# TensorE takes a task between the last pooled products of a pair and the next skip term, and tables of steps and shares change with it

## The chip, the cores and the metric

The kernel runs on one core of one Trainium2 chip. The core has TensorE (PE, matmuls), VectorE (DVE), ScalarE (ACT), GpSimd (POOL) and SyncE (SP, which issues most DMAs here). Each works through its own list of instructions in order, and they meet at semaphores. The metric is the device time of one execution in microseconds (us); lower is better.

## What is computed

The reference is one layer of a network on x of 2 sequences x 2048 rows x 512 features, in float32:

```python
h = _layernorm(x) * (1 + ca) + sa
x = x + ga * mixer(h)
h = _layernorm(x) * (1 + cb) + sb
x = x + gb * ffn(h)            # one 512 x 512 product, the sum of 8 factors, and a bias

# mixer, E = 1024 channels, N = 16 states, 4 taps
h, gate = split(h @ in_proj_w.T)
h = silu(conv4(h) + conv_b)                  # along the sequence
dt, Bp, Cp = split(h @ x_proj_w.T)           # 128, 16 and 16 columns
dt = softplus(dt @ dt_proj_w.T + dt_proj_b)
s[t] = s[t-1] * exp(dt * A) + (dt * h) * Bp  # the scan, for each channel and state
y = sum over states of s * Cp
y = (y + h * D) * silu(gate)
return y @ out_proj_w.T
```

## The kernel before

**Rounds, units, quads, pairs and steps.** The rows are cut into 16 chunks of 256 rows, and a round works on one chunk (8 chunks for each sequence). A round scans 1024 channels x 16 states. A unit is one state of a pair of channel tiles (128 partitions x 2 x 256 rows). There are 64 units in a round: 4 pairs (`q`) of 16 units. Four units make a quad, two units make a step `s`, so a round has 32 steps and 16 quads, and a pair has 8 steps. Pairs begin at steps 0, 8, 16 and 24.

**A unit's way through the engines.** ACT writes exp(dt * A) into one of three PSUM banks (`decays`, L722). POOL has made the inputs of a whole quad (`make_ub`, L568). DVE scans (`scan`, L1426). The state is then multiplied by C. A table gives each quad the number of its units that POOL multiplies (`EVEN_POOL` for even chunks, `ODD_POOL` for odd ones; `FIRST_POOL`, `FOLD_POOL` and `LAST_POOL` for chunks 0, 1 and 15). These are the last units of the quad: DVE scans them into `state_p`, and POOL multiplies them in one instruction for the quad (L596). The others stay in the bank, and DVE multiplies them into the ring `sc_d` (L1441). ACT copies the last column of every state to `carry` (L706) before the bank is used again, and clears the bank's middle column (L718) where DVE had used the bank for a product. TensorE adds the products over the 16 states by transposing them into one PSUM bank, `y_bank` (L1010). A new pair starts that bank with the skip term h * D (`turn_skip`, L1001), and for that ACT must have copied the finished sums of the pair before it (`copy_y`, L811), which waits for POOL's last products of that pair to be turned.

**The two side streams.** Between the scans of round c the engines do the second half of chunk c-1 (gate, sums, output projection, FFN), which the code marks `lc`, and the first half of chunk c+1 (input projection, taps, dt, B and C), marked `la`. TensorE's part of them is in `one_round` (L1307 on): 

- `project_gate` (L1057) makes the gate's columns, ACT takes their tanh (`tanh_gate`, L859) and DVE multiplies (`silu_gate`, L1500).
- `turn_sums` (L1141) turns the sums of a pair, and DVE multiplies the gate by them (`gate_sums`, L1522).
- `project_out` (L1157) is the output projection, which DVE adds to x (`residual_mixer`, L1529).
- `project_h` (L1085) makes one of eight input tiles at the steps in `IN_AT`, two for each pair of channel tiles. With a pair complete, ACT copies it for the taps and applies the last tap and the bias (`copy_h`, L766 to L775), DVE adds one tap (`taps`, L1481), TensorE the other two (`add_tap`, L1068, `ADD_AT`), ACT takes the tanh (`tanh_before`, L787) and DVE multiplies (`silu_before`, L1490, both at `SILU_AT`). In the kernel before, `copy_h` on ACT and `taps` on DVE are both ruled by `TAP_AT`.

The second numbers of these tables hold for rounds 1 and later. The order of work on an engine is the order in which `one_round` of that engine calls these functions. Within a step of TensorE it is: `add_tap`, the turns of the products (`turn_states`), the side work for chunk c+1, the side work for chunk c-1. Within a step of ACT it is: the decays of two units, with `copy_y` and a few others between, then `skip`, the work for chunk c+1, and last `tanh_gate`. So `tanh_gate(3)` at step 5 stands behind `copy_h(0)` of the next chunk.

## Time and profile before

| | us |
|---|---|
| median of 3 runs | 2022.62 |
| lowest to highest | 2021.11 to 2022.76 |
| the profiled execution | 2025.55 |
| its span, first to last instruction | 2023.8 |
| first scan starts at (from the span's start) | 60.5 |
| rounds 2 to 14, start of the first to start of round 15 | 325.8 to 1878.1 |
| last scan starts at | 1992.5 |

Busy time in the span: DVE 1867.4 us (92%), POOL 1835.7 (91%), PE 1759.7 (87%), ACT 1517.1 (75%).

The rows further down are of this one execution. A row of the timeline says when an instruction (or a row of like ones, xcount) began, how long it was busy, and in square brackets how long its engine had been idle before it and whose work ended the idle time. Each DVE instruction is counted as busy some 0.09 us into the next one: scans that follow each other start 1.19 us apart, and a product 0.59 us before the next instruction. TensorE's groups overlap likewise: four transposes of one unit take 0.43 us from start to start, an input or gate tile 1.73, half an output row tile (L1157 x4) 1.72. Where these distances are used, they are differences of start times in the rows.

### The profile page before, as it was taken

Reading aid. Unit: us, or ns where it says so; the run is one execution under the profiler, and the core shown is the slowest. Engines: PE = TensorE matmul, PEld = TensorE weight load, DVE = VectorE, ACT = ScalarE, POOL = GpSimd, SP = SyncE. Lnnn points to the kernel's source line nnn. Section 1 sums busy time; section 2 is a strip of 40 time slices with the busy share of each in tenths; the row PEclk is TensorE's granted clock in tenths of the full one; section 3 lists DMA queues with packets and bytes.
Section 4 is the critical chain, followed back from the end, with each engine's and each line's share of the span. In section 5 each row is a group of like instructions: output and inputs, shape, how many; then the busy total and the mean of one; then the engine's idle time right before and its main releaser. Section 6 shows DMA issues by size and latency. Waiting matters only on the chain.

```text
span 2023.8 us, 29343 instructions
## 1 busy us (share of the span) xinstructions
PE 1759.7 (87%) x9128; PEld 1312.2 (65%) x9128; DVE 1867.4 (92%) x2240; ACT 1517.1 (75%) x4646; POOL 1835.7 (91%) x925
## 2 busy tenths in 40 slices
PE   7985889889889898988989888898988899898798
PEld 5664757667576765757666675766757576676564
DVE  2799989999999999999999999999999999999995
ACT  3767778697877869777786977878787786878662
POOL 1789999999999999999998999999999999999992
PEclk9897999999999999999999999999999999999798
DMA  4656514132140412304042240403223040311200
GB/s 171 235 114 153 140 48 147 31 121 79 43 143 15 152 47 97 103 30 154 17 141 68 111 141 22 157 22 131 68 73 121 28 156 22 121 53 55 92 27 32
DMA packets 72001, 186.17 MB, mean 92 GB/s; under 512 B 6818, under 2 KB 8482, under 8 KB 63908
## 3 DMA queue, kind: packets, MB, share of 16 engines
q1 hardware_dynamic: 68148, 176.95, 26.3%
q0 software_dynamic: 3696, 7.34, 2.2%
q8 instruction: 73, 1.20, 0.2%
q14 instruction: 84, 0.69, 0.1%
HBM read 172.20 MB, written 12.06 MB: 91 GB/s over the span
## 4 chain that ended last, share of the span: by engine, by line
PE 42%; ACT 19%; POOL 15%; DVE 13%; issue 9%; DMA 1%; DVEq 0%; POOLq 0%; SPq 0%; ACTq 0%
PE y_bank L1010 10%; PE bank_a L1085 10%; PE bank_c L1157 9%; POOL ub L568 8%; ACT decay L722 7%; DVE decay L1426 5%; POOL state_p L596 5%; PE bank_c L1057 4%; DVE state_p L1426 3%; PE bank_a L1068 2%; ACT dt L835 2%; DVE sc_d L1441 2%; ACT L722 2%; ACT hT L737 2%; ACT L835 2%
## 5 line engine op out<-in xcount | busy, mean ns | idle before, releaser
L568 POOL TENSOR_TENSOR ub<-u,b_all 128x2048 f32<-128x2048 f32 x255 | 1160.4, 4551 | 48.5 <-DMA b_all<-bc_scratch 47.4
L722 ACT ACTIVATE decay<-dt,decay_rate 128x256 f32<-128x256 f32 (+1 forms) x2048 | 889.6, 466 | 36.0 <-DVE state_p L1426 34.3
L1426 DVE TENSOR_TENSOR_SCAN decay<-decay,carry,ub 128x512 f32<-128x512 f32 x610 | 763.7, 1277 | 25.8 <-ACT decay L722 23.8
L596 POOL TENSOR_TENSOR state_p<-state_p,c_all 128x1024 f32<-128x1024 f32 (+1 forms) x256 | 498.7, 1948 | 85.3 <-ACT carry L706 82.4
L1426 DVE TENSOR_TENSOR_SCAN state_p<-decay,carry,ub 128x512 f32<-128x512 f32 x414 | 527.4, 1274 | 9.3 <-ACT decay L722 7.2
L1010 PE MATMUL y_bank<-ident,sc_d 128*128 128x128 f32 x2440 | 362.5, 283 | 79.9 <-DVE sc_d L1441 79.5
L1441 DVE TENSOR_TENSOR sc_d<-decay,c_all 128x512 f32<-128x512 f32 x610 | 406.7, 671 | 0.0
L1010 PEld LDWEIGHTS y_bank<-ident,sc_d 128*128 128x128 f32 x2440 | 292.9, 145 | 146.1 <-DVE sc_d L1441 120.8
L706 ACT ACTIVATE carry<-decay 128x2 f32<-128x2 f32 x610 | 100.8, 165 | 264.8 <-DVE sc_d L1441 262.9
L1010 PEld LDWEIGHTS y_bank<-ident,state_p 128*128 128x128 f32 x1656 | 195.7, 143 | 126.9 <-POOL state_p L596 71.7
L1010 PE MATMUL y_bank<-ident,state_p 128*128 128x128 f32 x1656 | 231.0, 279 | 53.2 <-POOL state_p L596 52.0
L1085 PE MATMUL bank_a<-hT,win_h 128*128 128x256 f32 x992 | 240.5, 387 | 32.4 <-DVE hc L1490 30.0
L1057 PE MATMUL bank_c<-hT,win_z 128*128 128x256 f32 x960 | 230.7, 387 | 0.0
L1157 PE MATMUL bank_c<-wo,yg 128*128 128x512 f32 x480 | 223.8, 594 | 0.0
L1085 PEld LDWEIGHTS bank_a<-hT,win_h 128*128 128x128 f32 x992 | 182.3, 193 | 58.7 <-DVE hc L1490 35.7
L1057 PEld LDWEIGHTS bank_c<-hT,win_z 128*128 128x128 f32 x960 | 181.7, 196 | 22.6
L1068 PE MATMUL bank_a<-pre_z,tap_diag 128*128 128x256 f32 x496 | 120.4, 386 | 12.2 <-DVE bank_a L1481 12.2
L1157 PEld LDWEIGHTS bank_c<-wo,yg 128*128 128x128 f32 x480 | 86.6, 191 | 67.0 <-issue 64.8
L1068 PEld LDWEIGHTS bank_a<-pre_z,tap_diag 128*128 128x128 f32 x496 | 92.7, 191 | 39.8 <-DVE bank_a L1481 15.8
L1187 PE MATMUL bank_c<-ffn,hT 128*128 128x512 f32 x240 | 115.9, 605 | 0.0
L1001 PE MATMUL y_bank<-ident,skipped 128*128 128x128 f32 x256 | 42.9, 294 | 71.5 <-ACT y_rows L811 71.5
L718 ACT ACTIVATE decay<-ident 128x1 f32<-128x1 f32 x608 | 103.4, 170 | 0.1
(139 smaller groups left out, 1842.1 us busy)
## 6 DMA issues: line engine op xcount, KB each, us to landing
win_h<-win_m SPq DMA_DIRECT2D x128, 256.0 KB, 2.6
win_z<-win_m SPq DMA_DIRECT2D x128, 256.0 KB, 2.8
b_all<-bc_scratch SPq DMA_DIRECT2D x31, 1024.0 KB, 4.7
c_all<-bc_scratch SPq DMA_DIRECT2D x31, 1024.0 KB, 6.6
xa<-x SPq DMA_DIRECT2D x16, 512.0 KB, 5.0
xc<-x SPq DMA_DIRECT2D x16, 512.0 KB, 3.8
out<-xc SPq DMA_DIRECT2D x15, 512.0 KB, 4.0
ffn<-factors POOLq DMA_DIRECT2D x7, 1024.0 KB, 10.0
```

The lines of the kernel that those rows point to most:

```text
L568: pool.tensor_tensor(ub[:, slot, :, :, :], u[:, (PAIRS * c + q) % U_PAIRS, :, :].unsqueeze(1).to_broadcast([P, QUAD, 2, ROWS]), b_all[:, n ...
L596: pool.tensor_tensor(part, part, c_all[:, n + QUAD - k:n + QUAD, :].unsqueeze(2).to_broadcast([P, k, 2, ROWS]), ALU.mult).then_inc(pooled, 1)
L718: act.activation(bk[:, ROWS:ROWS + 1], ident[:, 0:1], ACT.Copy, scale=0.0)
L722: last = act.activation(bk[:, j * ROWS + j:(j + 1) * ROWS], dt[:, pair % DT_PAIRS, j, j:], ACT.Exp, scale=decay_rate[:, e, n:n + 1])
L1010: last = pe.matmul(y_bank[:, at:at + P], tile[:, j, t * P:(t + 1) * P], ident[:, :], start=False, stop=last_of_pair, is_transpose=True, sk ...
L1057: last = pe.matmul(dst[:, j * ROWS:(j + 1) * ROWS], tile[:, k, :], hTc[:, k, :], start=(k == 0), stop=(k == KD - 1))
L1068: last = pe.matmul(h_lane(c, q)[:, j * ROWS:(j + 1) * ROWS], tap_diag[:, i, 2 * q + j, :], pre[q % 2][:, j, k:k + ROWS], start=False, stop ...
L1085: last = pe.matmul(h_lane(c, q)[:, j * ROWS:(j + 1) * ROWS], win_h[i % H_TILES][:, k, :], hT[c % H_RING][:, k, :], start=(k == 0 and j == ...
L1157: last = pe.matmul(bank_c[t][:, :], yg[:, k, t * P:(t + 1) * P], wo[:, k, :], start=(k == 0), stop=(k == KE - 1))
L1187: last = pe.matmul(bank_c[t][:, :], hT[c % H_RING][:, k, t * P:(t + 1) * P], ffn[:, k, :], start=False, stop=(k == KD - 1))
L1426: dve.tensor_tensor_scan(dst, bk[:, :], ub[:, quad % UB_RING, i, :, :].rearrange("p j r -> p (j r)"), carried_in[:, n, 2 * q:2 * q + 1], A ...
L1441: dve.tensor_tensor(sc_d[:, i % D_RING, :, :], bk[:, :].rearrange("p (j r) -> p j r", j=2), c_all[:, n:n + 1, :].to_broadcast([P, 2, ROWS] ...
```

## The change

Six things change; the number of instructions of each kind is the same.

1. On TensorE `turn_states` is split. The turn of POOL's products of the quad before (`turn_finished`) comes first. At steps 1, 9, 17 and 25, where a pair ends, one task follows it before the skip term: `project_gate(c-1, 2, 1)`, `project_out(c-1, 0, 0)`, `project_dt(c+1, 1)`, and the bias with the first product of `project_ffn(c-1, 1)`. At step 0 the gate tile also comes ahead of the turns.
2. In the rest of a step TensorE does the work for chunk c-1 ahead of that for chunk c+1, where it was the other way round.
3. In rounds 1 and later the first four input tiles come a step earlier (steps 1 to 4 for 2 to 5).
4. On ACT `tanh_gate` comes right behind the step's decays.
5. `copy_h` gets a table of its own, equal to the old `TAP_AT`. DVE's taps of pairs 2 and 3 come a step later (12 and 14), TensorE's too (13 and 15), and the tanh and silu that follow (15 and 17).
6. The tables of POOL's share are spread otherwise: quads 3 and 7 (the last of pairs 0 and 1) go from 2 to 1, quad 12 from 1 to 2, in even chunks quad 8 from 2 to 3, in odd chunks quad 4 from 1 to 2. The sums stay 27 and 26 units.

```diff
-IN_AT = ((2, 3, 4, 5, 7, 8, 9, 10), (2, 3, 4, 5, 8, 9, 10, 11))
...
+IN_AT = ((2, 3, 4, 5, 7, 8, 9, 10), (1, 2, 3, 4, 8, 9, 10, 11))
+COPY_AT = ({5: 0, 7: 1, 10: 2, 12: 3}, {5: 0, 7: 1, 11: 2, 13: 3})
+TAP_AT = ({5: 0, 7: 1, 10: 2, 12: 3}, {5: 0, 7: 1, 12: 2, 14: 3})
...
-EVEN_POOL = (2, 2, 2, 2, 2, 2, 2, 2, 2, 2, 2, 1, 1, 1, 1, 1)
...
+EVEN_POOL = (2, 2, 2, 1, 2, 2, 2, 1, 3, 2, 2, 1, 2, 1, 1, 1)
...
                     decays(2 * step + 1)
...
+                    if lc is not None and s in (1, 3, 5):
+                        tanh_gate(c - 1, {1: 1, 3: 2, 5: 3}[s])
...
-                        if a in TAP_AT[c > 0]:
-                            copy_h(c + 1, TAP_AT[c > 0][a])
+                        if a in COPY_AT[c > 0]:
+                            copy_h(c + 1, COPY_AT[c > 0][a])
...
+            def turn_finished(step):
+
+                quad = step // 2
+                if step % 2 and quad:
+                    turn_on_pool(quad - 1)
+
             def turn_states(step):
 
                 quad = step // 2
                 first = quad % (N // QUAD) == 0
-                if step % 2 and quad:
-                    turn_on_pool(quad - 1)
...
+                    turn_finished(STEPS * c + s)
+                    if lc is not None:
+                        if s <= 1:
+                            project_gate(c - 1, 2, s)
+                        if s == 9:
+                            project_out(c - 1, 0, 0)
+                        if s == 25:
+                            ffn_bias(c - 1, 1)
+                            project_ffn(c - 1, 1, (0,))
+                    if la is not None and s == 17:
+                        project_dt(c + 1, 1)
                     turn_states(STEPS * c + s)
```

What the order of the instructions shows follows for round 4, an even one. The numbers behind the names are those of the buffers; in these rows a transposed unit is x4.

TensorE from step 9 to step 11, at the start of pair 1, before (L1085 is an input tile, L1157 the output projection, L1001 the skip term, `state_p` POOL's products, `sc_d` DVE's):

```order
L1010 MATMUL y_bank<-ident,state_p 128x128 x8
L1001 MATMUL y_bank<-ident,skipped 128x128 x4
L1010 MATMUL y_bank<-ident,sc_d 128x128 x8
L1085 MATMUL bank_a0<-hT2,win_h0 128x256 x4
L1157 MATMUL bank_c0<-wo,yg 128x512 x2
L1010 MATMUL y_bank<-ident,sc_d 128x128 x4
L1085 MATMUL bank_a1<-hT2,win_h1 128x256 x4
L1157 MATMUL bank_c0<-wo,yg 128x512 x2
L1010 MATMUL y_bank<-ident,state_p 128x128 x8
L1010 MATMUL y_bank<-ident,sc_d 128x128 x4
L1085 MATMUL bank_a1<-hT2,win_h2 128x256 x4
L1157 MATMUL bank_c0<-wo,yg 128x512 x2
```

The same place in the changed kernel, whose lines are 1 to 5 further down (L1011, L1002, L1090, L1162):

```order
L1011 MATMUL y_bank<-ident,state_p 128x128 x4
L1162 MATMUL bank_c0<-wo,yg 128x512 x2
L1002 MATMUL y_bank<-ident,skipped 128x128 x4
L1011 MATMUL y_bank<-ident,sc_d 128x128 x8
L1090 MATMUL bank_a0<-hT2,win_h0 128x256 x4
L1011 MATMUL y_bank<-ident,sc_d 128x128 x4
L1162 MATMUL bank_c0<-wo,yg 128x512 x2
L1090 MATMUL bank_a1<-hT2,win_h1 128x256 x4
L1011 MATMUL y_bank<-ident,state_p 128x128 x8
L1011 MATMUL y_bank<-ident,sc_d 128x128 x4
L1162 MATMUL bank_c0<-wo,yg 128x512 x2
L1090 MATMUL bank_a1<-hT2,win_h2 128x256 x4
```

The first output projection stands ahead of the skip term, POOL's part is one unit instead of two, and the last input tile (L1090, win_h2) has three output projections ahead of it in this piece instead of two.

DVE from step 12 to step 14, before (L1426 scan, L1441 product, L1481 the tap of pair 3, L1490 the silu of pair 2):

```order
L1426 SCALAR_TENSOR_TENSOR decay1<-decay1,carry0,ub 128x512
L1426 SCALAR_TENSOR_TENSOR decay2<-decay2,carry0,ub 128x512
L1441 TENSOR_TENSOR sc_d<-decay1,c_all 128x512
L1426 SCALAR_TENSOR_TENSOR state_p<-decay0,carry0,ub 128x512
L1441 TENSOR_TENSOR sc_d<-decay2,c_all 128x512
L1426 SCALAR_TENSOR_TENSOR state_p<-decay1,carry0,ub 128x512
L1481 SCALAR_TENSOR_TENSOR bank_a1<-pre_z,conv,bank_a1 128x256 x2
L1426 SCALAR_TENSOR_TENSOR decay0<-decay0,carry0,ub 128x512
L1426 SCALAR_TENSOR_TENSOR decay2<-decay2,carry0,ub 128x512
L1441 TENSOR_TENSOR sc_d<-decay0,c_all 128x512
L1490 SCALAR_TENSOR_TENSOR hc<-tanh_s,bank_a0 128x512
```

And in the changed kernel (L1438, L1453 and L1493 are the scan, the product and the tap):

```order
L1438 SCALAR_TENSOR_TENSOR decay2<-decay2,carry0,ub 128x512
L1438 SCALAR_TENSOR_TENSOR decay0<-decay0,carry0,ub 128x512
L1453 TENSOR_TENSOR sc_d<-decay2,c_all 128x512
L1493 SCALAR_TENSOR_TENSOR bank_a0<-pre_z,conv,bank_a0 128x256 x2
L1438 SCALAR_TENSOR_TENSOR state_p<-decay1,carry0,ub 128x512
L1453 TENSOR_TENSOR sc_d<-decay0,c_all 128x512
L1438 SCALAR_TENSOR_TENSOR state_p<-decay2,carry0,ub 128x512
L1438 SCALAR_TENSOR_TENSOR decay1<-decay1,carry0,ub 128x512
L1438 SCALAR_TENSOR_TENSOR decay0<-decay0,carry0,ub 128x512
L1453 TENSOR_TENSOR sc_d<-decay1,c_all 128x512
L1493 SCALAR_TENSOR_TENSOR bank_a1<-pre_z,conv,bank_a1 128x256 x2
```

The tap of pair 3 went from ahead of step 14's first scan to the end of step 14, and the tap of pair 2 from step 11 to step 12.

ACT at step 5, from the decays of unit 11 on, before (L766 to L775 are `copy_h(0)`, L859 is `tanh_gate(3)`):

```order
L722 ACTIVATE decay1<-dt,decay_rate 128x255
L766 ACTIVATE pre_z<-hist0 128x2x3
L767 ACTIVATE pre_z<-bank_a0 128x2x256
L770 ACTIVATE hist0<-bank_a0 128x6
L775 ACTIVATE bank_a0<-bank_a0,conv 128x256 x2
L859 ACTIVATE tanh_s<-bank_c1 128x512
L722 ACTIVATE decay0<-dt,decay_rate 128x256
```

ACT at the same place in the changed kernel (L860 is `tanh_gate(3)`, L767 to L776 are `copy_h(0)`):

```order
L723 ACTIVATE decay1<-dt,decay_rate 128x255
L860 ACTIVATE tanh_s<-bank_c1 128x512
L767 ACTIVATE pre_z<-hist0 128x2x3
L768 ACTIVATE pre_z<-bank_a0 128x2x256
L771 ACTIVATE hist0<-bank_a0 128x6
L776 ACTIVATE bank_a0<-bank_a0,conv 128x256 x2
L723 ACTIVATE decay0<-dt,decay_rate 128x256
```

The tanh moved from behind the copies to ahead of them. At step 13 ACT's rows are the same in both kernels: `copy_h(3)`, and right behind it the decays of unit 28.

## Rows read from the trace of the kernel before

**Rows 1.** Windows view, rounds 2 to 14: length, busy us (instructions), clock, DMA.

```profile
325.80:1878.10 1552.30, 1375.38 (x7336) 1037.46 (x7334) 1491.44 (x1783) 1224.10 (x3753) 1473.49 (x736) 0.99 0.26 86
```

**Rows 2.** Waits view, DVE, rounds 2 to 14: us in total, times, longest us.

```profile
DVE yg L1500 <- ACT tanh_s L859: 15.6, 13, 1.9
DVE xc L1529 <- PE bank_c L1157: 12.3, 13, 0.9
DVE decay L1426 <- ACT decay L722: 11.9, 33, 1.3
DVE bank_a L1481 <- ACT bank_a L775: 9.5, 13, 0.9
DVE yg L1522 <- PE bank_c L1141: 5.3, 13, 0.4
```

**Rows 3.** Timeline of DVE, round 7 (from 921.2): start, busy us, [idle before].

```profile
942.40 0.69 DVE L1500 SCALAR_TENSOR_TENSOR yg<-tanh_s,bank_c 128x512 f32<-128x512 f32 x1 [1.89 <-ACT tanh_s L859]
...
956.34 0.68 DVE L1490 SCALAR_TENSOR_TENSOR hc<-tanh_s,bank_a 128x512 f32<-128x512 f32 x1
...
974.44 0.88 DVE L1481 SCALAR_TENSOR_TENSOR bank_a<-pre_z,conv,bank_a 128x256 f32<-128x256 f32 x2 [0.67 <-ACT bank_a L775]
975.23 2.47 DVE L1426 TENSOR_TENSOR_SCAN decay<-decay,carry,ub 128x512 f32<-128x512 f32 x2
...
989.88 0.69 DVE L1529 TENSOR_TENSOR xc<-bank_c,xc 128x512 f32<-128x512 f32 x1 [0.95 <-PE bank_c L1157]
```

**Rows 4.** Timeline of PE in round 7, steps 8 to 16.

```profile
957.07 1.99 PE L1085 MATMUL bank_a<-hT,win_h 128*128 128x256 f32 x8 [2.15 <-DVE hc L1490]
958.90 1.04 PE L1010 MATMUL y_bank<-ident,state_p 128*128 128x128 f32 x8
960.71 0.63 PE L1001 MATMUL y_bank<-ident,skipped 128*128 128x128 f32 x4 [0.78 <-ACT y_rows L811]
961.18 1.47 PE L1010 MATMUL y_bank<-ident,sc_d 128*128 128x128 f32 x12
962.49 1.89 PE L1085 MATMUL bank_a<-hT,win_h 128*128 128x256 f32 x8
964.22 1.88 PE L1157 MATMUL bank_c<-wo,yg 128*128 128x512 f32 x4
...
972.42 1.88 PE L1157 MATMUL bank_c<-wo,yg 128*128 128x512 f32 x4
...
986.24 3.60 PE L1157 MATMUL bank_c<-wo,yg 128*128 128x512 f32 x8
```

**Rows 5.** Timeline of ACT in round 7, step 13 and the decays behind it.

```profile
972.62 0.21 ACT L766 ACTIVATE pre_z<-hist 128x6 f32<-128x6 f32 x1 [0.70 <-PE bank_a L1085]
...
974.33 0.87 ACT L722 ACTIVATE decay<-dt,decay_rate 128x256 f32<-128x256 f32 x2
```

**Rows 6.** Timeline of PE at pair 0's start: round 6, then round 7.

```profile
811.09 1.89 PE L1057 MATMUL bank_c<-hT,win_z 128*128 128x256 f32 x8
...
928.17 0.63 PE L1001 MATMUL y_bank<-ident,skipped 128*128 128x128 f32 x4 [2.04 <-ACT y_rows L811]
...
930.08 3.00 PE L1057 MATMUL bank_c<-hT,win_z 128*128 128x256 f32 x8
```

**Rows 7.** Timeline of DVE in round 6 at step 5.

```profile
822.34 0.69 DVE L1500 SCALAR_TENSOR_TENSOR yg<-tanh_s,bank_c 128x512 f32<-128x512 f32 x1 [0.40 <-ACT tanh_s L859]
```

**Rows 8.** Timeline of PE in round 3 at step 8.

```profile
478.46 3.60 PE L1085 MATMUL bank_a<-hT,win_h 128*128 128x256 f32 x8 [2.14 <-DVE hc L1490]
```

**Rows 9.** Windows view of that stretch, columns as in rows 1.

```profile
478.00:482.00 4.00, 3.54 (x9) 2.84 (x10) 4.00 (x6) 1.41 (x5) 4.00 (x3) 0.57 0.00 0
```

**Rows 10.** Timeline of DVE: round 1 at step 26, then round 7 at step 22.

```profile
305.32 1.29 DVE L1426 TENSOR_TENSOR_SCAN decay<-decay,carry,ub 128x512 f32<-128x512 f32 x1 [0.95 <-ACT decay L722]
...
1004.59 2.47 DVE L1426 TENSOR_TENSOR_SCAN decay<-decay,carry,ub 128x512 f32<-128x512 f32 x2 [0.40 <-ACT decay L722]
```

**Rows 11.** Waits view, POOL, rounds 2 to 14.

```profile
POOL state_p L596 <- ACT carry L706: 57.9, 55, 2.8
```

More of the change, by code:

```diff
@@ L57 @@
 DT_PAIRS = 5
-EVEN_POOL = (2, 2, 2, 2, 2, 2, 2, 2, 2, 2, 2, 1, 1, 1, 1, 1)
-ODD_POOL = (2, 2, 2, 2, 1, 2, 2, 2, 2, 2, 2, 1, 1, 1, 1, 1)
+EVEN_POOL = (2, 2, 2, 1, 2, 2, 2, 1, 3, 2, 2, 1, 2, 1, 1, 1)
+ODD_POOL = (2, 2, 2, 1, 2, 2, 2, 1, 2, 2, 2, 1, 2, 1, 1, 1)
 FIRST_POOL = (2, 2, 1, 1, 1, 1, 1, 2, 1, 1, 1, 1, 1, 1, 1, 1)
@@ L1322, in one_round @@
                             pe.wait_ge(rows_made, 2 * BATCH)
[L1323 to L1338 removed]
                     if lc is not None:
[L1340 to L1341 removed]
+                        if s in (2, 3):
+                            project_gate(c - 1, 3, s - 2)
                         if 4 <= s <= 7:
                             turn_sums(c - 1, s - 4)
[L1344 to L1345 removed]
+                        if 10 <= s <= 12:
                             project_out(c - 1, 0, s - 9)
@@ L1365, in one_round @@
                             project_ffn(c - 1, 1, (3,))
+                    if la is not None:
+                        if c == 0 and s == 3:
+                            turn_x(1, 0)
+                            turn_x(1, 1)
+                        if a in IN_AT[c > 0]:
+                            i = IN_AT[c > 0].index(a)
+                            project_h(c + 1, i // 2, i % 2)
+                        if s in (16, 18, 19):
+                            project_dt(c + 1, s - 16)
+                        if s in (18, 19):
+                            project_b_c(c + 1, s - 18)
+                        if s == 20:
+                            project_b_c(c + 1, 2)
+                            project_b_c(c + 1, 3)
+                        if s in (22, 23, 26, 27):
+                            expand_dt(c + 1, s - 22 - 2 * (s // 26))
                     if c + 2 < CHUNKS and s == 31:
```

30 lines of the change are left out of this document (2 added, 28 removed).

## The prediction

> **What bounds the kernel now.** I read the windows view first. In rounds 2 to 14 DVE is busy 1491.4 of 1552.3 us, and its line in the waits view adds up to nearly all of the rest, so a round of 119.4 us is DVE's own work plus DVE's waits [rows 1, 2]. A change that moves work and adds none can gain only from these waits. There are 55.9 us of them over 13 rounds, 4.3 in a round, and the timeline says where they stand [rows 2, 3]:
> - Step 5, the third gate product waits for ACT's tanh: 15.6 us in all, 1.89 in one kind of round and 0.40 in the other [rows 2, 3, 7].
> - Step 6, a gate sum waits for TensorE: 5.3 us [rows 2].
> - Step 13, the tap of pair 3 waits for ACT's copy: 9.5 us [rows 2, 3].
> - Step 17, the second residual waits for TensorE's output projection: 12.3 us, 0.95 in each round [rows 2, 3].
> - Scans that wait for decays: 13.2 us, of which 4.2 stand at step 10 and 7.8 at steps 22 and 23, and one of 1.3 in round 14 [rows 2, 10]. (The line of 11.9 and one more of 1.3; I sorted them by the number of scans ahead of them.)
>
> POOL waits 57.9 us for ACT's carries in the same rounds and never holds a scan up, since no line of DVE's waits names it [rows 2, 11].
>
> **Part 1: the tanh ahead of the copies (step 5), and gate work first on TensorE.** In round 6 the copies took ACT 1.7 us ahead of the tanh, as they do at step 13 (972.62 to 974.33), and DVE waited 0.40 [rows 5, 7]. With the tanh first, it is done 1.7 us sooner and the 0.40 is gone. In round 7 the wait was 1.89. There TensorE's gate tile at step 1 took 2.83 us from start to start (3.00 busy) against 1.72 (1.89 busy) in round 6, behind an idle gap of 2.04 at the skip term [rows 6]; it and the gap held back the input tile that ACT's copy waits for. The input tiles come one step earlier now and the gate tile goes into the gap, so both parts of the 1.89 go: 15.6 us in 13 rounds. The copy behind the tanh then ends about when DVE has done the gate product, 0.59 after its start; I take nothing for it and up to 0.3 us a round as bound. At step 6 the turned sums no longer stand behind input tiles (1.73 each), so the 5.3 goes. Half of the 4.2 at step 10 or more goes with POOL's lighter quad 3: ACT's copy of the sums waited there for a turn of two units that is now one, 0.43 sooner; I take all of it.
>
> **Part 2: from step 8 to step 17.** Here TensorE works without a gap from the first silu on: the input tile begins 0.05 us after the silu ends (957.02, that is 956.34 + 0.68), and the last output projection ends as the residual begins, 32.9 us later [rows 3, 4]. The gap at the skip term is 0.94 us from start to start (the turn of two units takes 0.87, 958.90 to 960.71 is 1.81) [rows 4]. The output projection (1.72) fills it, and TensorE's end moves to 31.9 after the silu. That alone would be worth 0.94 a round. But the order shows something that works against it: the eighth input tile at step 11 now stands behind a third output projection. Before, it ended at 972.42, which is 15.40 after the silu [rows 4]. Now 1.72 more are ahead of it, 0.94 less of gap, and 0.43 less of POOL's turn (quad 3 has one unit; in odd rounds quad 4 has one unit less for DVE's turns and one more for POOL's, which cancels): 15.40 + 1.72 - 0.94 - 0.43 = 15.75. ACT copies at step 13 only when this tile is there; it had already waited 0.70 for it [rows 5]. ACT's copy takes 1.71, and right behind it in ACT's list are the decays of unit 28, 0.87 more [rows 5]. So the scan of unit 28 can't begin before 15.75 + 0.20 + 1.71 + 0.90 = 18.56 after the silu; in the kernel before it was 18.21 (975.23) [rows 3]. The tap of pair 3 used to stand ahead of that scan and covered its wait, with 0.67 of waiting and 0.79 of work from 974.44 to 975.23 [rows 3]. It has moved behind, and so has nothing to cover with. DVE arrives at the scan at 18.21 - 0.67 - 0.79 - 0.59 (one product less in quad 4) = 16.16 in odd rounds, and at 18.21 - 0.67 - 0.79 - 0.50 (the wait at step 10) = 16.25 in even ones. **A new wait of about 2.3 us** takes the place of the one of 0.73, under another name: a scan that waits for ACT's decays. From there to the residual DVE had 13.7 us of work (975.23 to 989.88 less 0.95) [rows 3]. It gets the tap (+0.79) and quad 7's third product (+0.59), and the last silu goes behind the residual (-0.59); even rounds lose a product in quad 8 (-0.59). The residual then begins at 32.5 in even and 33.0 in odd rounds, later than TensorE's 31.9. So the wait of 0.95 at step 17 goes, and TensorE's saving at the gap is worth nothing there.
>
> The Trainium skill, TensorE: Matmul & The Clock Gate, "Architectural detail", says that ScalarE and VectorE are strict FIFOs. It speaks against putting work ahead of the eighth tile; without it ACT could make the decays while it waits for the tile, and the sum would be 1975.7 us. The trace agrees with the rule: the decays behind ACT's 0.70 wait began only when the copies were done [rows 5].
>
> **Part 3: the rest.** TensorE's gaps at steps 17 and 25 and ACT's stall behind the copy of the sums at step 18 get shorter, but no wait of DVE follows them, so they are worth nothing. The last silu at step 17 adds 0.59 behind the residual, and quad 12's second pooled unit takes 0.59 off. The 0.6 a round at steps 22 and 23 stays: ACT has the same list there [rows 10]. Quads 3 and 7 now have three DVE products in a row; the row nearest to that is step 22, where such a quad begins and waits 0.40 plus 0.20 [rows 10]. In quads 3 and 7 DVE also has gate sums, taps or a silu between its scans, which gives ACT time, so I take 0, with 0.6 a quad as the bound. POOL's three units in quad 8 cost it one more unit, and it has 57.9 / 13 = 4.5 us a round of waits [rows 11].
>
> **Sum.** Gone in rounds 2 to 14: 15.6 + 5.3 + 4.2 + 9.5 + 12.3 = 46.9 us. New: 13 x 2.3 = 29.9. Net 17.0. Round 0 has other tables, rounds 1 and 15 and the tail I take as unchanged. Of the profiled execution (2025.55, span 2023.8) this makes 2008.5; the median of the runs lies 2.9 below the profiled one, so **2022.6 - 17.0 = 2005.6 us**. The terms can move it by 4 for 0.3 a round at step 5, 5 for 0.4 in the new wait, 3 in round 1: 1996 to 2015.
>
> **Rivals.**
> - *The new wait does not come, and TensorE bounds the stretch.* If the eighth tile is not as late as worked out (the taps' order or ACT's lead may differ), the residual begins at TensorE's 31.9. DVE would reach it after 30.2 us in even rounds (32.9 less waits of 2.1, less 0.59) and 30.7 in odd ones, so it waits 1.5 on average, 19.9 in all: 46.9 - 19.9 = 27, **1995.6**. For: the 0.35 us by which the scan moves is small. Against: ACT's list at step 13 is the same, and that chain already set the scan.
> - *The clock's fall moves into the stretch that TensorE bounds.* In 7 of the 13 rounds the slow gate tile of rows 6 stands behind the 2.04 gap. With that gap filled, the longest gap is the 2.15 at step 8 [rows 4]. It happened there once: in round 3 the input tile behind it took 3.60 busy instead of 1.99 at a mean granted clock of 0.57, so mostly at the lower level of 1.2 GHz instead of 2.4, 1.6 us lost [rows 4, 8, 9]. Seven such rounds cost 11.2: **2016.8**. Against: one in 13 so far. The same page of the Trainium skill says in its Part 1 that the default is throttled and that activity releases it, which makes idle gaps the cause, as rows 6 and 8 do.
> - *Quads 3 and 7 stall (the other side).* A bank that held a DVE product is free only when ACT has copied its carry and cleared it. If ACT can't keep pace in the two new quads of three products, each costs the 0.6 of rows 10, 15.6 in all: 2021.2, no change. In round 1 a scan waited 0.95 in such a stretch [rows 10]. At 0.95 a quad it is 24.7: **2030.3**, slower. It turns slower from 0.81 a quad, (2026.7 - 2005.6) / 26. For: ACT has the skip and the copies at steps 6 and 7. Against: DVE's extras there.
> - *POOL becomes the bound.* Its waits of 4.5 us are for ACT's carries. If they stay where they are, the round stays at 119.4: **2022**.
>
> **Chances.** A measurement can tell about 0.2%, 4.0 us. Forecast 0.46, TensorE's bound 0.17, clock 0.15 (all three faster: 0.78); quads 3 and 7 0.16, of which 0.07 is within 0.2% and 0.09 slower; POOL 0.06, the same. Faster 0.78, same 0.13, slower 0.09. The range reaches over the first three cases with their bounds and to the edge of no change: 1989 to 2022.
>
> **What would show it.** In the waits of DVE, the lines for `yg` on the tanh and on TensorE's turned sums and for the tap on ACT's copy vanish. The line of scans on ACT's decays grows from 11.9 to some 35 us, with the new entries at the first scan of step 14. The residual's wait goes to 0; if it stays near 1.5 a round and step 14 has no wait, the first rival holds. Slow tiles at a clock below 1 at step 8 show the second, waits at steps 7 to 9 and 15 to 17 the third. TensorE's 0.78 at the skip terms of steps 9 and 17 should be gone in any case. It would all be wrong if DVE had come to wait for something that has no line now, such as POOL's inputs.

## The result, and the profile after

The changed kernel takes **2043.43 us** (median of 4 runs, 2036.58 to 2049.72) against 2022.69 (2021.11 to 2022.83) for the kernel before on the same chip: ratio 1.0102, 95% interval 1.0076 to 1.0128. It is slower by 1%, where 2005.6 was forecast and 2022 was the end of the range. Its profiled execution is its fastest, 2036.58 (span 2034.8), and the 15.4 us by which rounds 2 to 14 grew can be placed in it (1567.70 against 1552.30). The whole profiled execution grew by only 11.0, since what lies outside these rounds, which the forecast took as unchanged, is 4.4 shorter. One execution of the run with the old tables of POOL's share further down took 3837 us and is left out of that run's median. In this section line numbers are those of the changed kernel: L1438 is the scan, L1453 DVE's product, L1493 the tap, L1541 the residual, L1011 the turns, L1002 the skip term, L1090 an input tile, L1128 the expansion of dt.

The windows view of rounds 2 to 14 (length; busy us and instructions of PE, PEld, DVE, ACT, POOL; clock) answers to [rows 1]:

```profile
324.60:1892.30 1567.70, 1395.18 (x7334) 1042.66 (x7333) 1488.17 (x1783) 1224.52 (x3752) 1473.73 (x735) 0.98 0.26 85
```

DVE does the same work (1488.2 us, it was 1491.4). PE does the same work too and is busy 20 us more, at a mean clock of .98 instead of .99. DVE's waits over the same rounds answer to [rows 2]:

```profile
DVE decay L1438 <- ACT decay L723: 56.5, 55, 1.8
DVE state_p L1438 <- ACT decay L723: 19.4, 17, 2.4
```

The four lines of `yg`, `xc` and `bank_a` are gone, as forecast. What is left are scans that wait for decays, 75.9 us in all where some 35 were forecast and 55.9 was the total before. DVE's timeline of round 7 (step 10, step 14, the second residual at step 17, step 25) answers to [rows 3]:

```profile
970.77 1.29 DVE L1438 TENSOR_TENSOR_SCAN decay<-decay,carry,ub 128x512 f32<-128x512 f32 x1 [0.80 <-ACT decay L723]
...
986.04 2.47 DVE L1438 TENSOR_TENSOR_SCAN decay<-decay,carry,ub 128x512 f32<-128x512 f32 x2 [1.84 <-ACT decay L723]
...
1000.45 0.66 DVE L1541 TENSOR_TENSOR xc<-bank_c,xc 128x512 f32<-128x512 f32 x1
...
1029.43 1.28 DVE L1438 TENSOR_TENSOR_SCAN state_p<-decay,carry,ub 128x512 f32<-128x512 f32 x1 [0.98 <-ACT decay L723]
```

And PE's timeline, first round 4 at step 8 and at step 18, then round 7 at step 18:

```profile
600.97 2.71 PE L1090 MATMUL bank_a<-hT,win_h 128*128 128x256 f32 x8 [2.15 <-DVE hc L1502]
...
640.71 1.12 PE L1011 MATMUL y_bank<-ident,sc_d 128*128 128x128 f32 x4 [3.11 <-DVE sc_d L1453]
641.62 1.92 PE L1107 MATMUL bank_a<-hc,xp 128*128 128x256 f32 x4
...
1006.22 0.66 PE L1011 MATMUL y_bank<-ident,sc_d 128*128 128x128 f32 x4 [3.27 <-DVE sc_d L1453]
1006.72 1.03 PE L1107 MATMUL bank_a<-hc,xp 128*128 128x256 f32 x4
```

At that place the kernel before had a gap of 0.42 us, here its round 7:

```profile
995.14 0.66 PE L1010 MATMUL y_bank<-ident,sc_d 128*128 128x128 f32 x4 [0.42 <-DVE sc_d L1441]
```

The same instruction at step 18 (a turn x4, then a projection x4) takes 0.66 and 1.03 us in round 7 and 1.12 and 1.92 in round 4, twice the time at the same size. The windows view of the two stretches in round 4 has the granted clock in the column behind the busy times:

```profile
600.90:604.40 3.50, 3.43 (x13) 2.89 (x14) 3.50 (x5) 0.87 (x2) 3.50 (x2) 0.67 0.00 0
640.70:645.30 4.60, 4.59 (x12) 2.46 (x12) 4.60 (x7) 4.55 (x15) 4.52 (x4) 0.50 0.00 0
```

0.50 is the lower of TensorE's two levels, 1.2 GHz instead of 2.4, and 0.67 a mixture of both. Each such **fall of the clock** in rounds 2 to 14 comes behind a gap of TensorE. I cut a round into three stages: from its first scan to the end of the first silu at step 8 (stage 1), from there to the second residual (stage 2), and from the residual to the end of the last scan (stage 3). They show what a fall costs, since rounds of one kind, even or odd, differ in little else:

| us | before | changed |
|---|---|---|
| stage 1, no fall | 34.17 | 33.79 |
| stage 1, fall behind the 2.04 gap of step 1 | 35.85 (7 rounds of 13) | none |
| stage 2, no fall | 32.87 | 32.34 even, 32.94 odd |
| stage 2, fall behind the 2.15 gap of step 8 | 34.47 (1 round) | 34.02 even, 34.62 odd (9 rounds) |
| stage 3, no fall | 50.27 | 50.87 (50.82 to 51.13 in 6 rounds) |
| stage 3, fall behind the gap of 3.11 or 3.27 at step 18 | none | 52.1 to 53.7 (7 rounds) |

Summed over the 13 rounds: the clock took 11.8 + 1.6 = 13.4 us before and takes 9 x 1.68 = 15.1 at step 8 and 13.6 at step 18 now, 15.3 more. All the rest together (-4.9 in stage 1, -3.2 in stage 2, +8.3 in stage 3) is 0.2. So in this reading the order of the work gained nothing, and the clock lost all of the 15.4. The experiments put both halves to the test.

### The profile page after: what moved, and what is told of

The parts are those of the page before. It is cut to its first block and busy times, and to the rows that moved or that the text cites. A ratio compares the mean times of both kernels' runs of the same rounds, so it can differ in the third digit from the quotient of the medians.

```text
span 2034.8 us, 29343 instructions
## 1 busy us (share of the span) xinstructions
PE 1773.9 (87%) x9128; PEld 1310.7 (64%) x9128; DVE 1864.1 (92%) x2240; ACT 1517.3 (75%) x4646; POOL 1836.4 (90%) x925
## 5 line engine op out<-in xcount | busy, mean ns | idle before, releaser
L1438 DVE TENSOR_TENSOR_SCAN decay<-decay,carry,ub 128x512 f32<-128x512 f32 x610 | 764.2, 1277 | 70.8 <-ACT decay L723 68.7
L597 POOL TENSOR_TENSOR state_p<-state_p,c_all 128x1024 f32<-128x1024 f32 (+2 forms) x256 | 498.6, 1948 | 98.1 <-ACT carry L707 89.3
L1438 DVE TENSOR_TENSOR_SCAN state_p<-decay,carry,ub 128x512 f32<-128x512 f32 x414 | 526.4, 1273 | 25.2 <-ACT decay L723 24.4
L1011 PE MATMUL y_bank<-ident,sc_d 128*128 128x128 f32 x2440 | 360.0, 279 | 154.3 <-DVE sc_d L1453 154.1
L1011 PEld LDWEIGHTS y_bank<-ident,sc_d 128*128 128x128 f32 x2440 | 282.5, 142 | 213.7 <-DVE sc_d L1453 194.8
L1453 DVE TENSOR_TENSOR sc_d<-decay,c_all 128x512 f32<-128x512 f32 x610 | 407.3, 670 | 2.5 <-PE y_bank L1011 2.5
L1011 PE MATMUL y_bank<-ident,state_p 128*128 128x128 f32 x1656 | 237.9, 284 | 45.6 <-POOL state_p L597 45.4
L1090 PE MATMUL bank_a<-hT,win_h 128*128 128x256 f32 x992 | 246.1, 393 | 32.4 <-DVE hc L1502 30.0
L1011 PEld LDWEIGHTS y_bank<-ident,state_p 128*128 128x128 f32 x1656 | 200.8, 146 | 104.5 <-POOL state_p L597 63.2
L1090 PEld LDWEIGHTS bank_a<-hT,win_h 128*128 128x128 f32 x992 | 188.9, 196 | 74.3 <-DVE hc L1502 35.7
L1162 PE MATMUL bank_c<-wo,yg 128*128 128x512 f32 x480 | 229.8, 607 | 0.0
L1062 PE MATMUL bank_c<-hT,win_z 128*128 128x256 f32 x960 | 226.1, 381 | 0.0
L1062 PEld LDWEIGHTS bank_c<-hT,win_z 128*128 128x128 f32 x960 | 175.1, 191 | 19.7
L1162 PEld LDWEIGHTS bank_c<-wo,yg 128*128 128x128 f32 x480 | 86.3, 198 | 67.7 <-issue 67.7
L1073 PEld LDWEIGHTS bank_a<-pre_z,tap_diag 128*128 128x128 f32 x496 | 92.6, 191 | 33.3 <-issue 13.4
L546 POOL TENSOR_TENSOR u<-dt,hc 128x512 f32<-128x512 f32 x63 | 80.4, 1276 | 0.0
```

The lines of the kernel that those rows point to most:

```text
L597: pool.tensor_tensor(part, part, c_all[:, n + QUAD - k:n + QUAD, :].unsqueeze(2).to_broadcast([P, k, 2, ROWS]), ALU.mult).then_inc(pooled, 1)
L1011: last = pe.matmul(y_bank[:, at:at + P], tile[:, j, t * P:(t + 1) * P], ident[:, :], start=False, stop=last_of_pair, is_transpose=True, sk ...
L1062: last = pe.matmul(dst[:, j * ROWS:(j + 1) * ROWS], tile[:, k, :], hTc[:, k, :], start=(k == 0), stop=(k == KD - 1))
L1073: last = pe.matmul(h_lane(c, q)[:, j * ROWS:(j + 1) * ROWS], tap_diag[:, i, 2 * q + j, :], pre[q % 2][:, j, k:k + ROWS], start=False, stop ...
L1090: last = pe.matmul(h_lane(c, q)[:, j * ROWS:(j + 1) * ROWS], win_h[i % H_TILES][:, k, :], hT[c % H_RING][:, k, :], start=(k == 0 and j == ...
L1162: last = pe.matmul(bank_c[t][:, :], yg[:, k, t * P:(t + 1) * P], wo[:, k, :], start=(k == 0), stop=(k == KE - 1))
```

## The experiments

The theory at the start: the time was lost to falls of the clock, and a fall belongs to the gap before it. The first rival: the falls come with the chip or the run, and the new waits of DVE (steps 14 and 25) are the loss. The means is a filler: TensorE transposes a tile of zeros into a sum that is open, which adds nothing to it and makes a gap shorter. Ratios are to runs of the kernel before on the same chip (medians of 2021.4 to 2023.9 on the three chips used), with the 95% interval in brackets; where two experiments stand side by side, they may be of different chips. Line numbers are those of each run's own kernel: the scan is L1450 in one and L1454 in another.

**Both gaps of the changed kernel filled.**

```
+                    if la is not None and s == 8:
+                        add_zeros(y_bank, 16)
+                    if la is not None and s == 17:
+                        add_zeros(y_bank, 24)
```

where `add_zeros` is, in short, `pe.matmul(bank[:, 0:P], zero, ident, start=False, stop=False, is_transpose=True)` in a loop.

> The changed kernel with TensorE kept busy in two of its gaps: 16 transposes of a tile of zeros, added to the sums of the pair (which they leave as they are), at the end of step 8's turns, and 24 at the end of step 17's, in rounds 0 to 14. Clock theory: the changed kernel loses its time to falls of TensorE's clock behind the gaps of 2.15 us at step 8 (9 of 13 rounds, 1.7 us each) and of 3.1 us before step 18's turn (7 of 13 rounds, 1.2 to 2.7 us each). Without them a round is 117.3 us as in its undisturbed rounds instead of 120.6, so the whole is 43 us less than the profiled 2036.6: 1990 to 2000 us, no slow tile at steps 8 and 18 in rounds 2 to 14. Order theory (the lists of ACT and TensorE alone cost the time): no gain, 2036 to 2050 us or a little more for the added work.

Measured: **2011.5 us** (2010.65 to 2012.3), ratio .9939 [.9924, .9954], and no fall in rounds 2 to 14. 32 us came off the changed kernel by work that computes nothing, and the rounds are those that had no fall before (33.78, 32.33 or 32.93, 50.87 to 51.14), so these stages show no other effect of the filler. The waits of DVE at steps 14 and 25 stayed, here over rounds 2 to 14:

```profile
DVE decay L1450 <- ACT decay L725: 33.5, 39, 1.8
DVE state_p L1450 <- ACT decay L725: 15.2, 13, 2.4
```

48.7 us, of which 24.0 at step 14 and 15.2 at step 25. So the fillers are worth 32 us in the median (more than the 15.3 of the profiled execution, which was the fastest of four; the others had a clock of .966, .963 and .960). My lower figure of 1990 to 2000 missed, since I had added the three stages up and left out the 1.1 us between a round's last scan and the next round's first.

**Only the gap of step 8 filled** (the first two lines of that diff).

> The same filler at step 8 alone. Clock theory: the falls at step 8 go (9 x 1.7 = 15 us), those behind the 3.1 us gap at step 18 stay and may be more: 2015 to 2030 us, the stretch from the first silu to the second residual is 32.3 us in even and 32.9 in odd rounds in every round. Order theory: no gain.

Measured: **2027.7 us** (2022.82 to 2029.23), 1.0016 [1.0007, 1.0025]. There was no fall at step 8 any more, but there were falls at step 18 in 12 of 13 rounds, where the unfilled kernel had 7. Round 7, which had none there, now reads:

```profile
995.52 1.12 PE L1013 MATMUL y_bank<-ident,sc_d 128*128 128x128 f32 x4 [3.27 <-DVE sc_d L1463]
996.43 1.91 PE L1115 MATMUL bank_a<-hc,xp 128*128 128x256 f32 x4
```

**The kernel before, its gap of step 1 filled** (`add_zeros(bank_c[0], 16)` ahead of the skip term). This is what the change itself does to that gap, and nothing else.

> The kernel before with its gap of 2.04 us at step 1 filled: 16 transposes of zeros ahead of the skip term of pair 0, added to a gate tile, in rounds 1 to 15. Clock theory: the 7 slow gate tiles of rounds 2 to 14 go, 1.5 us each, 10.7 us: 2012 us, if the fall does not move to the gap of 2.15 us at step 8, where each costs 1.6; if it moves there in 9 of 13 rounds, 2022.7 + 14.4 - 10.7 = 2026 us. Order theory: within 2 us of 2022.7.

Measured: **2023.0 us** (2020.35 to 2025.55), .9999 [.9989, 1.0008]. The gap is gone and so are its falls, and they come back at step 8 in 8 of 13 rounds. Round 7, first the skip term [rows 6], then step 8 [rows 4]:

```profile
928.09 0.63 PE L1003 MATMUL y_bank<-ident,skipped 128*128 128x128 f32 x4 [0.29 <-ACT y_rows L813]
...
955.32 2.98 PE L1095 MATMUL bank_a<-hT,win_h 128*128 128x256 f32 x8 [2.15 <-DVE hc L1500]
```

The gap of 2.15 had stood there before, and the tile behind it took 1.99. It takes 2.98 now. A gap that cost nothing in this round cost 1.7 us as soon as an earlier one was closed. The number of falls did not change: the eight rounds (3, 5, 7, 8, 10, 11, 13, 14) are the seven that had one at step 1 and the one that had it at step 8.

**The kernel before, both its gaps filled** (the same, and 16 zeros at step 8).

> The kernel before with both gaps filled: 16 transposes of zeros ahead of the skip term of pair 0 and 16 at the end of step 8's turns. Theory (the clock is the difference between the two kernels, their lists of work are worth the same): no slow tile in rounds 2 to 14, every round 34.2 + 32.9 + 50.3 us in its three stretches, against 33.8 + 32.6 + 51.0 in the changed kernel with its gaps filled, so the whole is within 3 us of that kernel's 2011.5: 2009 to 2014. Rival (the order of the changed kernel has a gain of its own that the clock hides): 2018 or more. Second rival (the fall moves to a third gap): 2015 to 2023, with slow groups at steps 17 to 23.

Measured: **2011.8 us** (2009.69 to 2014.29), .9952 [.9937, .9967], no fall. Here the two orders of work stand side by side without the clock: 2011.8 for the old one and 2011.5 for the new one, on two chips. The ratios (.9952 and .9939) have intervals that overlap, and rounds 2 to 14 take 1538.7 and 1540.0 us. The change is worth nothing clear of the noise when the clock is taken out, as the sum of 0.2 said. The first rival does not explain the loss, but the question moves: four waits went, and where did their gain go?

**The old tables of taps** (`TAP_AT`, `ADD_AT` and `SILU_AT` of before in the changed kernel, no filler).

> The changed kernel with the old tables for the taps, their TensorE part and the silu (11 and 13, 12 and 14, 14 and 16). If the tap of pair 3 covered ACT's late decays, as the prediction has it: the wait at the first scan of step 14 falls from 1.8 us a round to about 1.0 on ACT's copy at step 13, the stretch from the first silu to the second residual in rounds without a fall of the clock is 0.6 to 0.8 us shorter (31.6 in even, 32.2 in odd rounds), and the whole is 8 to 10 us less, 2027 to 2040 us by the number of clock falls. If the place of the tap does not matter: the stretch stays at 32.3 and 32.9 and the time at 2036 to 2050 us.

Measured: **2024.7 us** (2022.61 to 2028.89), 1.0008 [.9999, 1.0017]. The gap of step 18 shrank from 3.1 and 3.3 to between 2.3 and 2.8, and falls there went from 7 rounds to 2; at step 8 there were 8, and one at step 23 behind a gap of 2.03. The tap again covers the wait for the eighth input tile (1.50 at the tap in place of 1.85 at the scan), and stage 2 is 32.15 and 32.75. I had expected 31.6 and 32.2, because I forgot that the last silu then stands ahead of the residual again.

**`project_h` ahead of `project_out` at steps 10 and 11**, in the changed kernel with both gaps filled:

```
+                    early_h = la is not None and lc is not None and s in (10, 11)
+                    if early_h:
+                        i = IN_AT[1].index(s)
+                        project_h(c + 1, i // 2, i % 2)
...
-                        if a in IN_AT[c > 0]:
+                        if a in IN_AT[c > 0] and not early_h:
```

> The changed kernel with both gaps filled and, at steps 10 and 11, the input tile ahead of the output projection again. Theory: the wait of 1.85 us at the first scan of step 14 comes from the eighth input tile, which stands behind one more projection; the tile now ends 1.72 sooner, that wait falls to 0.1 to 0.3, and TensorE's last output projection bounds the stretch instead: the second residual begins 31.9 us after the first silu in even and odd rounds (32.3 and 32.9 before), with a wait of 0.7 to 1.2 at step 17. 0.75 us a round, 10 in all: 2000 to 2004 us. Rival (the wait at step 14 comes from ACT's other work): it stays at 1.85 and the time at 2011.5.

Measured: **2005.1 us** (2004.59 to 2006.07), .9919 [.9904, .9933]. The wait at step 14 is gone and TensorE bounds stage 2 at 31.90 in every round:

```profile
DVE state_p L1454 <- ACT decay L725: 17.5, 13, 2.8
DVE xc L1557 <- PE bank_c L1170: 12.0, 13, 1.2
DVE decay L1454 <- ACT decay L725: 9.8, 28, 0.4
```

That confirms the chain of Part 2 (eighth tile, copy, decays, scan) and prices it: 6.4 us for what stood in the forecast as a wait of 29.9. In the traces stage 2 lost 9.2 us over 13 rounds, and stage 3 took 2.8 of them back, in even rounds: the wait at step 25 grew from 15.2 to 17.5 us.

**The old tables of POOL's share** (both of before), in the changed kernel with both gaps filled.

> The changed kernel with both gaps filled and the old tables of POOL's share. Theory: the second pooled unit of quad 12 leaves DVE without work to cover ACT's softplus at step 25 (a wait of 1.17 us a round that the kernel before does not have); with the old tables that wait goes, and the first scan of step 14 waits about 0.4 more since quad 3's turn on TensorE takes 0.43 more: 0.6 a round less in all, 2002 to 2006 us against 2011.5. Rival (the new tables help, as the lighter last quads bring the sums sooner): slower than 2013.

> The changed kernel with filled gaps and the old tables of POOL's share once more, for its waits: the time of the first runs (2004.7) again. If the table is what lengthens the wait at step 25, it is 0.1 to 0.4 us a round here (1.17 with the new tables), and the first scan of step 14 waits 2.2 instead of 1.85.

Measured: **2004.7 us** (2002.66 to 2005.12), .9914 [.9897, .993]; the trace read here is of the second run of the same kernel, 2003.9. Stage 1 is 33.18 instead of 33.79, one product of DVE (0.59) less in quad 3, and the wait at step 25 is 6.0 us instead of 15.2. The spread of POOL's share that the change brought costs 7 us.

**Quad 12's second unit given to quad 11**, in the changed kernel with both gaps filled, the old taps and `project_h` first.

> The changed kernel with both gaps filled, the input tile first at steps 10 and 11, the old tables for taps, TensorE's taps and silu, and the second pooled unit in quad 11 instead of quad 12. If all theories hold they add up to the point at which TensorE bounds the stretch between steps 8 and 17 (31.9 us less what the silu behind the residual had hidden, so 0.2 to 0.6 more than with the tile alone) and the wait at step 25 (1.17) and those at step 22 (0.39) go: 1990 to 1998 us. If ACT's list is the limit wherever DVE gets lighter, the waits come back at other steps and it is 2000 to 2006.

Measured: **2005.0 us** (2002.93 to 2008.7), .992 [.9904, .9936], a miss. In round 6 PE waited for POOL's products at step 23, the clock fell, and ACT waited for the expansion of dt; round 10 has the same fall. The two cost some 8 us of stage 3 in this execution, the slowest of four. In the other rounds the wait at step 25 is 0.6 or 1.1 us, where `project_h` first alone had 1.0 or 1.6, and new ones of 0.4 to 0.8 stand at step 23, as the second case of the expectation has it. PE's turn, ACT's second softplus, then DVE's scan:

```profile
887.41 1.73 PE L1013 MATMUL y_bank<-ident,state_p 128*128 128x128 f32 x8 [2.27 <-POOL state_p L599]
```

```profile
895.74 0.84 ACT L838 ACTIVATE dt<-bank_a,ch 128x256 f32<-128x256 f32 x2 [4.72 <-PE bank_a L1136]
```

```profile
898.91 1.28 DVE L1454 TENSOR_TENSOR_SCAN state_p<-decay,carry,ub 128x512 f32<-128x512 f32 x1 [4.91 <-ACT decay L725]
```

**Both of the costly parts taken out, gaps filled** (`project_h` first, old taps, old POOL tables; what is left is the task between, the tanh first, the work for chunk c-1 first on TensorE elsewhere, and the earlier input tiles), **and the same without filler.**

> The changed kernel with both gaps filled, the input tile first at steps 10 and 11, and the old tables for POOL's share, the taps and the silu. What is left of the change is the task between POOL's last products and the skip term, the earlier tanh and the earlier input tiles. Theory: the gate stages cost 33.2 us (quad 3's product is back on POOL), TensorE bounds the stretch from the first silu to the second residual at 31.9 + 0.4 (two units in quad 3's turn) = 32.3, the rest 50.3 as in the kernel before. 115.8 + 1.1 a round against 118.46 in the changed kernel with filled gaps: 1988 to 1996 us. Rival (ACT's list at steps 12 to 14 and 22 to 25 takes back what DVE saves): 2000 or more.

> The same without any filler. Clock theory: the lists are better, but the gaps of 2.1 us at step 8 and 2 to 3 us at step 18 are open, so the clock falls in most rounds at one of them: 8 to 13 rounds x 1.7 us at step 8 and some at step 18, 12 to 30 us more than with the filler: 2003 to 2022 us. Order theory: within 3 us of the kernel with the filler.

Measured: **1996.8 us** (1996.53 to 1997.38), .987 [.9855, .9884], and 2013.8 (2009.44 to 2015.1), .995 [.9931, .9969]. The stages are 33.18, 31.90 and 51.1 to 51.3. Without filler the clock falls at step 8 in 8 of 13 rounds again, and the median is 17 us longer; in the profiled executions rounds 2 to 14 are 12.0 longer (1537.8 against 1525.9).

**The part that the change is named after, alone** (`turn_finished` and one task ahead of the skip term at steps 1, 9, 17, 25, in the kernel before, nothing else):

```
+                    turn_finished(STEPS * c + s)
+                    if lc is not None:
+                        if s == 1:
+                            project_gate(c - 1, 2, s)
+                        if s == 9:
+                            project_out(c - 1, 0, 0)
...
```

> The kernel before with one part of the change alone: at steps 1, 9, 17 and 25 the gate tile, the output projection, the dt product and the bias with the first FFN product stand between the turn of POOL's products and the skip term. Tables, ACT's order and the order of the other work are the old ones. Theory: TensorE's gap of 0.78 at the skip terms of steps 9 and 17 and of 2.04 at step 1 go, but DVE is not faster for it: the input tiles at steps 9 to 11 stand 0.8 us later (1.72 less 0.94), so the stretch to the second residual keeps 32.7 us in even and odd rounds, and the fall of the clock moves from step 1 to step 8 in 6 to 10 rounds. 2018 to 2030 us. Rival (the gap was what cost): 0.94 us a round and the slow gate tiles, 10 to 25 us faster, 1998 to 2012.

Measured: **2008.2 us** (2008.03 to 2008.66), .9926 [.9911, .9941]: faster, where I had expected no gain. The stages are 33.95, 31.90 and 50.27, and the falls are as many as in the filled kernel before, 8 of 13 at step 8 (33.57). Part 2 had said so: "That alone would be worth 0.94 a round", and the table has 32.87 and 31.90.

**The same with 16 zeros at step 8.**

> The kernel before with the part that the change is named after alone (another task between POOL's last turns and the skip terms), and beside it sixteen transposes of zeros behind TensorE's turns of step 8, as a filler of the gap there. In the run of that part alone (2008.2 us) the clock fell at step 8 in 8 of 13 rounds, and a round with a fall was 1.67 us longer. Theory (these falls are all that the clock still takes): no fall in rounds 2 to 14, 8 x 1.67 = 13.4 us less, 1994 to 1996 us. Rival (a fall moves on to the next gap, as it did before): falls at steps 17 to 25, 2000 to 2008 us.

Measured: **1993.7 us** (1993.25 to 1995.49), .9857 [.9842, .9871], no fall. It came as the theory said, and the rival (the fall moves on) fell: no gap over 1.88 us is left in these rounds.

**Then the tanh ahead of the copies.**

```
+                    if lc is not None and s in (1, 3, 5):
+                        tanh_gate(c - 1, {1: 1, 3: 2, 5: 3}[s])
```

> The kernel just above, and tanh's gate right behind the decays on ScalarE, as the changed kernel has it. Theory (the wait of .57 us in the first stage of a round is tanh's): that stage falls from 33.95 to 33.4 us, 13 x .57 = 7.4 us, 1987 to 1989 us. Rival (the gate ahead delays ScalarE's later work by as much): the same time as the kernel above within 2 us.

Measured: **1999.9 us** (1999.54 to 2000.05), .9885 [.9869, .9902]. Neither case: 6.2 us slower. Round 7, ACT at step 5, then DVE's first tap:

```profile
931.18 0.60 ACT L861 ACTIVATE tanh_s<-bank_c 128x512 f32<-128x512 f32 x1 [1.36 <-PE bank_c L1069]
931.68 0.20 ACT L768 ACTIVATE pre_z<-hist 128x6 f32<-128x6 f32 x1
```

```profile
933.49 0.88 DVE L1503 SCALAR_TENSOR_TENSOR bank_a<-pre_z,conv,bank_a 128x256 f32<-128x256 f32 x2 [0.99 <-ACT bank_a L777]
```

The tanh waits 1.36 us for its gate tile, since TensorE still does input tiles first here, and the copies stand behind it on ACT. Stage 1 goes from 33.95 to 34.52. In the changed kernel the gate tile comes first, the tanh waits for nothing, and stage 1 has no wait at all. In the kernel of 1996.8 us, which has the tanh first, the gate first and the earlier input tiles, stage 1 takes 33.18. The tanh alone is a loss; which of the other two it needs was not tried apart.

**The expansion of dt ahead of the feed-forward work** at steps 22, 23, 26, 27, in the kernel of 1996.8 us.

```
+                    if la is not None and s in (22, 23, 26, 27):
+                        expand_dt(c + 1, s - 22 - 2 * (s // 26))
```

> The fastest kernel so far (1996.8 us: task between, tanh's gate first, input tiles earlier, filled gaps), with the expansions of dt ahead of the feed-forward work of the chunk before at steps 22, 23, 26 and 27 on TensorE. Its stage behind the residual takes 51.2 us, that of the part alone 50.3. Theory (that order on TensorE is what delays the second softplus): the stage is .9 us shorter, 13 x .9 = 11.7, about 1985 us. Half of it, if only the wait of .21 us at the second softplus goes: 1993 to 1995 us. Rival (ScalarE is late because its copy of dt waits 1.44 us for TensorE at step 21, further ahead): the stage stays at 51.2 us, 1996 to 1997 us.

Measured: **1991.2 us** (1990.69 to 1995.4), .9847 [.9832, .9862], **the fastest of all**, some 52 us below the changed kernel. ACT's softplus at step 25, first without the edit, then with it (one group of four, no wait between the halves):

```profile
1002.64 0.84 ACT L838 ACTIVATE dt<-bank_a,ch 128x256 f32<-128x256 f32 x2
1003.67 0.84 ACT L838 ACTIVATE dt<-bank_a,ch 128x256 f32<-128x256 f32 x2 [0.20 <-PE bank_a L1136]
```

```profile
998.77 1.28 ACT L838 ACT_TABLE_LOAD   x1
1000.07 1.57 ACT L838 ACTIVATE dt<-bank_a,ch 128x256 f32<-128x256 f32 x4
...
1001.77 1.28 ACT L725 ACT_TABLE_LOAD   x1
```

The waits at step 25 (7.9 us) went to 0 and stage 3 from 51.1 or 51.3 to 50.81. Of the 0.9 us a round between stage 3 of this kernel and of the part alone, 0.4 was this order. The other 0.5 stands at steps 22 and 23 (15.1 us of waits against 7.6) and stays open: ACT's copy of dt at step 21 waits 1.44 for TensorE there, and 0.32 with the part alone, but no run took that away by itself.

## Why the prediction was wrong, point by point

- **Part 1 was right in its waits, and counted the clock in them as a gain.** The waits for the tanh (15.6) and the turned sums (5.3) are gone and stage 1 has no wait. But the 15.6 were 13 x 0.40 and 7 x 1.49, and the second term, 10.4 us, came with the 7 falls of the clock, which I took for a cost of the gap that goes with it. In the kernel before with both gaps filled the same wait is 5.2. So 10.4 us were booked as gained which only moved. And stage 1 got only 0.38 us shorter (34.17 to 33.79), not 0.81: quad 3's third product, 0.59, is in it now. With the old tables it took 33.18.
- **The 4.2 at step 10** went in rounds without a fall. In the nine with a fall at step 8 this wait is 11.6 us in all, because the late input tile holds up everything behind it.
- **Part 2 was right in its chain and good in its sizes.** Step 14's wait came in all 13 rounds with 1.85 us, where 2.3 was forecast (24.0 us for 29.9), another 0.34 stands at step 12, and the residual begins at 32.34 and 32.94 where 32.5 and 33.0 were forecast. The waits of tap and residual went. In the run with `project_h` first, with the tile back at its place, the 24.0 went. The rule of strict FIFOs for ScalarE and VectorE (the Trainium skill, TensorE: Matmul & The Clock Gate, "Architectural detail") agrees with that: the decays had stood behind copies that waited for the tile. But what came of it was 6.4 us, since TensorE bounds that stage at 31.90, only 0.4 and 1.0 us sooner.
- **Part 3 failed, in two steps.** The first: "TensorE's gaps at steps 17 and 25 ... get shorter, but no wait of DVE follows them, so they are worth nothing". The time before a skip term got shorter, and the idle time came back at step 18 as 3.1 and 3.3 us. DVE reaches the residual 0.5 to 1.1 us after TensorE has ended its output, and then does the moved silu (0.59), so TensorE waits for DVE's product at step 18: 41.4 us in 13 rounds, 5.5 before. I had counted that DVE no longer waits for TensorE and stopped there. Who waits the other way round was the question, and 7 falls of the clock, 13.6 us, were the answer. In round 7 the gap is larger by 2.85: counted from the end of its last output projection, TensorE was ready 1.3 us earlier than before, and DVE's product came 1.55 later. The second: "quad 12's second pooled unit takes 0.59 off". DVE does arrive earlier, but at step 25 the scan waits for decays behind ACT's softplus and two table loads of 1.28 us. It waits 1.1 us a round (14.3 in all), and nothing was gained; the expansions that this softplus needs had been put behind feed-forward work by the same change. Steps 22 and 23, which were to stay at 0.6 a round, took 1.0.
- **The sum.** -17.0 was forecast, with nothing in it for the clock, and +0.2 is what the stages show apart from the clock. The two filled kernels, which have no falls in these rounds, show where the difference stands, as waits of DVE in rounds 2 to 14. The kernel before has 43.9 us of them without falls and had 55.9 with them, so 12.0 of the 46.9 counted as gone were the clock's. The new waits at steps 12 and 14 are 28.4 for the 29.9 forecast, and 2.7 at step 23 went that were to stay. The wait at step 25, for which the forecast had nothing, grew from 1.3 to 15.2. That makes 48.7 in the changed kernel, 4.8 more, where 5.0 less would have followed from the forecast's other terms. (The rounds are 1.3 us longer, 1540.0 against 1538.7; DVE's busy time is the smaller one in the changed kernel.)
- **The rivals.** "The clock's fall moves into the stretch that TensorE bounds" is what happened. It had the right mechanism and place and the right price (1.6 forecast, 1.68 measured), and was given 0.15 and the wrong argument: "Against: one in 13 so far". That count was taken while falls at step 1 came first. The run with the gap of step 1 filled had them in 8 of 13 at step 8 with the same gap of 2.15. Its 11.2 on top of the forecast was only the return of what the forecast had booked as a gain: the balance of moving alone is near nothing, as that run's 2023.0 shows. The new gap of step 18 was not in the rival at all. Of the other rivals none came: quads 3 and 7 did not stall, no line of DVE's waits names POOL, and TensorE's bound of 31.9 was not reached. (By that rival's own 30.2 and 30.7 its wait adds up to 19.1, not 19.9; nothing hangs on it.)
- **The other side.** The chance of slower (0.09) hung on one mechanism, quads 3 and 7. A bound for "a new gap of TensorE" could have been had from the rows: each fall 1.6, up to 13 rounds, two places.

The Trainium skill, TensorE: Matmul & The Clock Gate, says in its Part 1 that the default is throttled and that activity releases it. The trace agrees in direction: each fall stands behind idle time, and added work, even work on zeros, removed it (2008.2 to 1993.7 us for the named part).

## What to carry to other kernels

When a change moves work off or onto an engine that isn't the bound, write down that engine's idle gaps of before and after with their lengths, not only who waits for it; here the gap that grew from 0.4 to 3.1 and 3.3 us brought 7 falls of the clock, 13.6 us. A cost that comes in some rounds and not in others (1.68 us, 7 of 13) belongs to a cause of its own: take it out of the sum and ask where it will turn up next. And try the named part alone: it gave 15 us, and the five parts around it took that and more back. One of them, the tanh first, cost 6 us when it was added alone.

## What the runs showed of the hardware

- A fall of TensorE's clock to 0.50 stood, in rounds 2 to 14 of all the traces, only behind gaps of 2.03 us or more, and never behind the 13 gaps of 1.67 to 1.88 that each of these kernels has at step 31. Not every such gap was followed by one: of the 2.15 at step 8 none to nine of 13, depending on what came before in the round.
- Filling one gap moved the falls to the next: step 1 to step 8 (7 to 8 rounds), step 8 to step 18 (7 to 12). They ended when no gap over 1.9 was left, in eight kernels. The runs of the changed kernel lie 13 us apart (2036.6 to 2049.7) and the longer ones have the lower clock; those of the kernel of 1996.8 us, which has no falls there, lie within 0.9. Not all kernels without falls there agree so well: two others spread over 4.6 and 4.7 us.
- TensorE was busy 89% of rounds 2 to 14 (1395.18 of 1567.70) and still had 16 falls. A high mean share says nothing of them.
